# A table for the first-pass chunks, and small pieces spread over heads 1 to 3

## What is computed

```python
content = jnp.einsum('bqhd,bkhd->bhqk', q + u_bias, k)
pos_score = jnp.einsum('bqhd,khd->bhqk', q + v_bias, p)
pos_score = _rel_shift(pos_score)
score = (content + pos_score) / jnp.sqrt(jnp.float32(e))
attn = jax.nn.softmax(score, axis=-1)
ctx = jnp.einsum('bhqk,bkhd->bqhd', attn, v).reshape(b, s, e)
return ctx @ Wo + bo
```

## Time and profile before

| | |
|---|---|
| runs | 1982.84, 1982.9, 1983.7 us |
| profiled execution | 1981.65 us, its span 1979.9 us |
| TensorE busy | 1674.4 us, 85% |
| VectorE, ScalarE, POOL busy | 74%, 54%, 55% |
| attention loop | from about 100 to 1275 us of the span |
| granted TensorE clock, mean of the span | 0.892 |

### The profile page before, as it was taken

The page is one execution under the profiler, slowest core; times in us unless marked ns, Lnnn a source line. Parts: engine busy times, 40 slices in busy tenths (PEclk is TensorE's granted clock), DMA queues, the critical chain, the costliest instruction groups (busy, mean ns, idle before and its releaser), DMA issues. The chain is left out here.

```text
span 1979.9 us, 50794 instructions
## 1 busy us (share of the span) xinstructions
PE 1674.4 (85%) x12709; PEld 1283.0 (65%) x12710; DVE 1455.8 (74%) x5309; ACT 1068.1 (54%) x2080; POOL 1091.8 (55%) x2255
## 2 busy tenths in 40 slices
PE   3599999999999999999999999835444699999990
PEld 1366766766766766766766766634434599999990
DVE  4588788788788788788778788736555577777775
ACT  2067666666666666666666666501111465656553
POOL 4047546547547547547547547416877455555650
PEclk8599999999999999999999999955555799999995
DMA  4436436426426427327426426274221211111119
GB/s 167 127 95 155 107 85 159 110 77 164 112 70 172 111 64 177 109 64 174 109 71 167 109 81 165 75 236 116 65 65 42 67 53 52 51 53 53 52 49 257
DMA packets 167897, 212.14 MB, mean 107 GB/s; under 512 B 28049, under 2 KB 129313, under 8 KB 167681
## 3 DMA queue, kind: packets, MB, share of 16 engines
q1 hardware_dynamic: 137216, 149.63, 27.2%
q0 software_dynamic: 30464, 59.96, 12.2%
HBM read 127.01 MB, written 77.22 MB: 103 GB/s over the span
## 5 line engine op out<-in xcount | busy, mean ns | idle before, releaser
L778 DVE CUSTOM_DVE_ANT_0 junk<-pA,lmask 128x512 bf16<-128x512 f32 x1056 | 688.2, 683 | 224.5 <-PE pA L489 114.6
L720 ACT ACTIVATE prob<-pB 128x512 f32<-128x512 f32 x512 | 305.6, 597 | 194.0 <-PE pB L510 162.9
L722 ACT ACTIVATE prob<-pB 128x512 f32<-128x512 f32 x512 | 305.2, 596 | 1.3 <-PE pB L512 1.1
L489 PE MATMUL pA<-K,QL 96*128 96x512 f32 (+3 forms) x792 | 286.1, 363 | 19.9 <-DMA K<-split_operands 14.3
L528 PE MATMUL pC<-prob,vext 128*32 128x256 f32 x4112 | 283.8, 393 | 2.9 <-POOL prob L403 2.9
L403 POOL TENSOR_TENSOR prob<-prob,upper_diag 128x128 f32<-128x128 f32 x512 | 255.0, 498 | 47.8 <-POOL prob L398 10.5
L512 PE MATMUL pB<-QL,K 97*128 97x512 f32 (+3 forms) x768 | 279.4, 364 | 0.0
L510 PE MATMUL pB<-QU,K 97*128 97x512 f32 (+3 forms) x640 | 269.7, 421 | 7.4 <-ACT prob L720 2.8
L491 PE MATMUL pA<-K,QU 96*128 96x512 f32 (+3 forms) x660 | 235.9, 359 | 12.1 <-DVE acc L778 7.2
L396 POOL MEMSET prob<- 1x1 f32 x448 | 39.5, 88 | 345.6 <-ACT prob L722 345.5
L1471 POOL DMA_INDIRECT expert_rows<-yb,dst x144 | 158.2, 1098 | 102.5 <-DVE yb L1592 74.5
(11 more groups left out here) (272 smaller groups left out, 3437.7 us busy)
## 6 DMA issues: line engine op xcount, KB each, us to landing
QL<-split_operands SPq DMA_DIRECT2D x67, 256.0 KB, 3.5
QU<-split_operands SPq DMA_DIRECT2D x67, 256.0 KB, 3.9
K<-split_operands SPq DMA_DIRECT2D x67, 256.0 KB, 3.9
xg<-routed_rows SPq DMA_DIRECT2D x76, 130.0 KB
QL<-split_operands SPq DMA_DIRECT2D x67, 128.0 KB, 3.5
QU<-split_operands SPq DMA_DIRECT2D x67, 128.0 KB, 3.7
K<-split_operands SPq DMA_DIRECT2D x67, 128.0 KB, 3.7
split_operands<-c_h POOLq DMA_DIRECT2D x16, 512.0 KB, 6.4
```

The lines of the kernel that those rows point to most:

```text
L489: mm = pe.matmul(dst[:, 0:low], QL[0:KROWS, s, q], K[0:KROWS, s, k0:k0 + low], start=True, stop=True)
L720: act.activation(p[:, 0:HALF], pB[:, 0:HALF], ACT.Exp, scale=SCALE).then_inc(p_exp, 1)
L722: act.activation(p[:, HALF:S], pB[:, HALF:S], ACT.Exp, scale=SCALE).then_inc(p_exp, 1)
L778: v.tensor_tensor_reduce(junk[:, n % S1_BUFS, :], pA[n % S1_BUFS][:, :], lmask[:, at:at + HALF], 1.0, -3.0e38, ALU.add, ALU.max, acc[:, s, ...
```

## The change

The first-pass chunks of a unit are now taken from a table, `CHUNKS_AT`. In heads 0, 4, 5 and 7 (`PLAIN`) the nine units take 2, 1, 3, 2, 1, 3, 2, 3 and 1 chunks, in heads 1, 2, 3 and 6 (`EVEN`) two each. `ORDER` moves the diagonal chunk 16 to the third place of a head (unit 1) and 17 to the ninth (unit 4). Of an odd number above one, the rest goes behind the second half. The eight projections go from head 2's units 0 to 7 to the places of `PROJECT_AT`; "project 0/1", "shifted 0/1" and "values 0/1" move by one to four units, and what depends on them moves too: the splits, the positions, the stores and the swap.

```diff
-        M_ORDER.update({(1, 5): "project 1", (1, 7): "shifted 1", (6, 6): "values 0"})
-        W_ORDER = {(1, 0): "turn 0", (1, 2): "turn 1", (1, 4): "project 0", (1, 6): "shifted 0", (6, 5): "super", (6, 7): "values 1"}
+        M_ORDER.update({(1, 7): "project 1", (2, 2): "shifted 1", (6, 7): "values 0"})
+        W_ORDER = {(1, 0): "turn 0", (1, 2): "turn 1", (1, 5): "project 0", (2, 0): "shifted 0", (6, 5): "super", (7, 0): "values 1"}
+        PROJECT_AT = ((2, 3), (2, 5), (2, 7), (2, 8), (3, 0), (3, 2), (3, 3), (3, 5))
+        ORDER = (0, 1, 16, 2, 3, 4, 5, 6, 17, *range(7, 16))
+        EVEN, PLAIN = (2,) * S2U, (2, 1, 3, 2, 1, 3, 2, 3, 1)
+        CHUNKS_AT = {h: (EVEN if h in (1, 2, 3, 6) else PLAIN) for h in range(H)}
-        HIGH_AT = ((2, 5), (2, 6), (3, 0), (3, 1), (4, 1), (4, 2))
-        LOW_AT = ((2, 6), (2, 7), (3, 1), (3, 2), (4, 2), (4, 3), (4, 4), (4, 6))
+        HIGH_AT = ((3, 0), (3, 1), (3, 7), (3, 8), (4, 1), (4, 2))
+        LOW_AT = ((3, 1), (3, 2), (3, 8), (4, 0), (4, 2), (4, 3), (4, 4), (4, 6))
-        POSITIONS_AT = ((2, 7), (2, 8), (3, 1), (3, 3), (3, 5), (3, 7), (5, 2), (5, 4))
+        POSITIONS_AT = ((3, 3), (3, 4), (3, 6), (3, 7), (3, 8), (4, 0), (5, 2), (5, 4))
-        STORE_AT = {(3, 0): ("c", 0), (3, 2): ("c", 1), (3, 4): ("k", 0), (4, 4): ("gl", 0), (4, 7): ("gu", 0)}
+        STORE_AT = {(3, 5): ("c", 0), (4, 1): ("c", 1), (4, 2): ("k", 0), (4, 4): ("gl", 0), (4, 7): ("gu", 0)}
...
+        def chunks(h, u):
+
+            at, n = sum(CHUNKS_AT[h][:u]), CHUNKS_AT[h][u]
+            return [range(at, at + (n + 1) // 2), range(at + (n + 1) // 2, at + n)] if n < 3 else [range(at, at + 1), range(at + 1, at + n)]
...
+                    if h == 3:
+                        swap(b + 1)
                     if h == 2:
-                        swap(b + 1)
...
-                        second_pass(b, h, u, 0)
-                        first_pass(b, h + AHEAD, 2 * u)
-                        second_pass(b, h, u, 1)
-                        first_pass(b, h + AHEAD, 2 * u + 1)
-                        if (h, u) == (2, 0):
+                        for half in range(2):
+                            second_pass(b, h, u, half)
+                            for i in chunks(h, u)[half]:
+                                first_pass(b, h + AHEAD, i)
+                        if (h, u) == PROJECT_AT[0]:
                             pe.wait_ge(w_done, b * W_N + W_PRO + W_OF["shifted 0"] + 1)
-                        if h == 2 and u < PIECES:
-                            project(b + 1, u)
+                        if (h, u) in PROJECT_AT:
+                            project(b + 1, PROJECT_AT.index((h, u)))
...
-                        first_pass(b, h + AHEAD, 2 * u)
+                        first, *others = [i for half in chunks(h, u) for i in half]
+                        first_pass(b, h + AHEAD, first)
...
-                        first_pass(b, h + AHEAD, 2 * u + 1)
+                        for i in others:
+                            first_pass(b, h + AHEAD, i)
```

More of the change, by code:

```diff
@@ L475, in context_turned, with first_pass @@
                 return mm
-            def first_pass(b, h, n):
-                s = h % SLOTS
-                if n == 0:
+            def first_pass(b, h, i):
+                s, n = h % SLOTS, ORDER[i]
+                if i == 0:
                     pe.wait_ge(stk[s], b * (2 * STK) + (h // SLOTS + 1) * STK)
-                if not (isinstance(b, int) and h == 0 and n < S1_BUFS):
-                    pe.wait_ge(s1_read, b * (H * S1U) + h * S1U + n - S1_BUFS + 1)
-                dst = pA[n % S1_BUFS]
+                if not (isinstance(b, int) and h == 0 and i < S1_BUFS):
+                    pe.wait_ge(s1_read, b * (H * S1U) + h * S1U + i - S1_BUFS + 1)
+                dst = pA[i % S1_BUFS]
                 if n < NB * HPB:
@@ L492, in first_pass @@
                 else:
-                    for i in range(4):
-                        q = slice(P * (4 * (n % 2) + i), P * (4 * (n % 2) + i) + P)
-                        mm = pe.matmul(dst[:, P * i:P * i + P], QU[0:KROWS, s, q], K[0:KROWS, s, q], start=True, stop=True)
+                    for t in range(4):
+                        q = slice(P * (4 * (n % 2) + t), P * (4 * (n % 2) + t) + P)
+                        mm = pe.matmul(dst[:, P * t:P * t + P], QU[0:KROWS, s, q], K[0:KROWS, s, q], start=True, stop=True)
                 mm.then_inc(s1_ready, 1)
@@ L698, in _ @@
                         n = h * S2U + u
-                        if h == 2 and 0 < u <= PIECES:
-                            evacuate(b + 1, u - 1)
+                        before = (h, u - 1) if u else (h - 1, S2U - 1)
+                        if before in PROJECT_AT:
+                            evacuate(b + 1, PROJECT_AT.index(before))
                         if u == LATE:
@@ L706, in _ @@
                             act.activation(vext[:, :, H // 2:H, 0:D], held[:, :, :, :], ACT.Copy).then_inc(placed, 1)
-                        before = (h, u - 1) if u else (h - 1, S2U - 1)
                         if M_ORDER.get(before) in COPIES:
@@ L768, in super_out, with first_pass @@
                 v.tensor_tensor(acc[:, :, :, 3], src[:, 0:NB * H].rearrange("p (n h) -> p h n", h=H), cmask[:, :, :], ALU.add).then_inc(done, 1)
-            def first_pass(b, h, n):
-                s = h % H
-                pieces = known(v, b * (H * S1U) + h * S1U + n + 1)
+            def first_pass(b, h, i):
+                s, n, dst = h % H, ORDER[i], i % S1_BUFS
+                pieces = known(v, b * (H * S1U) + h * S1U + i + 1)
                 v.wait_ge(set_pool, POOL_SET)
@@ L777, in first_pass @@
                     at = 7 * P - P * qb + k0
-                    v.tensor_tensor_reduce(junk[:, n % S1_BUFS, :], pA[n % S1_BUFS][:, :], lmask[:, at:at + HALF], 1.0, -3.0e38, ALU.add, ALU.max,
+                    v.tensor_tensor_reduce(junk[:, dst, :], pA[dst][:, :], lmask[:, at:at + HALF], 1.0, -3.0e38, ALU.add, ALU.max,
                                            acc[:, s, qb, n % 2:n % 2 + 1]).then_inc(s1_read, 1)
@@ L781, in first_pass @@
                     g = n % 2
-                    for i in range(4):
-                        blk = 4 * g + i
-                        ttr = v.tensor_tensor_reduce(junk[:, n % S1_BUFS, P * i:P * i + P], pA[n % S1_BUFS][:, P * i:P * i + P], umask[:, :], 1.0, -3.0e38, ALU.add, ALU.max,
+                    for t in range(4):
+                        blk = 4 * g + t
+                        ttr = v.tensor_tensor_reduce(junk[:, dst, P * t:P * t + P], pA[dst][:, P * t:P * t + P], umask[:, :], 1.0, -3.0e38, ALU.add, ALU.max,
                                                      acc[:, s, blk, 2:3])
```

## The result

The changed kernel is **slower**: 2027.7 us median (2022.3 to 2037.7), the kernel before on the same chip 1982.9; ratio 1.0235, 95% interval 1.019 to 1.028. The forecast was 1958, the range 1938 to 1980. The profiled execution took 2029.55 us, its span 2027.9, mean granted clock 0.868 (before 0.892).

A forecast was written before the change was run, and what follows sets the result against it. It took VectorE to bound head 0 and an exp-and-matmul ring to bound quiet units without context. Terms of -2.55 us a batch, times 8, gave -20; clock -4; 1981.65 - 24.5 = 1957.2, median 1.25 higher: 1958, range 1938 to 1980.

The forecast's parts named there:

- I cost the stretch at nothing. The cover is VectorE's own backlog: Head 0 into head 1: VectorE is saturated, so the third chunks cost nothing; without that backlog the stretch would gain 0.5 us.
- 1.7 minus what the context of that unit hides is 1.1 net: Head 4: ScalarE's gl_h copy waits 1.7 us for POOL's position steps, 1.1 net; head 4 together +0.3 us.
- the clock falls at the new waits: Rival, chance 0.10: TensorE's fresh waits at (0,8) and (4,2) each cost 1.5 us a batch; 1977 us.
- The forecast's rule against it: Skill rule: idle gaps recurring in a loop re-throttle TensorE, so (0,8) and (4,2) would fall in every batch; 1977 us.
- clock term: Head 1: a third fewer clock drops expected, -4 us in all, bounds -9 and +12.
- The slower rival: Chance 0.12: the chain positions, gl, stores, stack becomes the loop's period; about 1994 us.
- stack wait of +0.6: Next batch's operands behind the gu store at (4,7): slack 0.7 us used up, +0.6 a batch charged, bounds 0 and 3.
- The pieces: Moved small pieces, us per batch: head 1 -1.4, head 2 -1.4, head 3 +1.4, values -0.25.
- The table in plain heads: Heads 0, 4, 5, 7: unit 8 -0.6, units 1 and 4 -0.2 each, read waits +0.55; a plain head gains about 0.5 us.
- The table in even heads: Heads 1, 2, 3, 6: unit 8 -0.4, units 1 and 4 +0.1 each; net -0.2 us a head.
- Wrong: Signs: head 5 unchanged, TensorE waiting over 2 us at head 6, gl_h over 4 us, or a lower mean loop clock.
- right: Signs: head 5 at most 15.4, its units 8 and 7 2.0 and 1.3; heads 1, 2, 3 19, 20.3, 19; gl_h waiting 1 to 2.

The follow-up runs named there:

- both repairs: Changed kernel with the residual add at (1,2) instead of (0,6), position steps at (3,3) to (3,8), first c store at (4,0): 1955.9 us, ratio 0.988.
- stores spread: Kernel with both repairs, its c stores put at (3,2) and (4,0) and its k store at (4,1): 1954.1 us, ratio 0.987.

## Why the prediction was wrong

- **"I cost the stretch at nothing. The cover is VectorE's own backlog"** (head 0): this step failed. I had the 2.61 us multiplication in the earlier trace rows and took it as its duration, though the addition of the same shape took 1.22. The 1.4 us between them was a meeting with POOL's residual add, whose place the table does not move but whose partner it does. After the change it meets the addition, with three reads and TensorE behind it. Cost: 7.6 us a batch in heads 0 and 1 (changed kernel against the one with the residual add moved). TensorE's stand, 2.76 us instead of 0.7, explains 2.1 of it; the rest came with the clock at 0.51 through the 12.67 us behind it. No run has the stand without the fall, so the two are not separated. The forecast had "about 1.2 us at (0,8)".
- **"1.7 minus what the context of that unit hides is 1.1 net"** (head 4): right mechanism, wrong size. Counted from the mask of (3,3) at 938.45, POOL took 16.2 us where 15.3 was summed (the upper select alone 1.54 for 1.1), and ScalarE stood at the copy after 13.2 instead of 13.6. The wait is 3.02 us, TensorE's share 2.26, and in five of eight batches the clock fell behind it. Head 4: +1.9 without the fall, +4.7 to +6.2 with it, forecast +0.3.
- **The rival "the clock falls at the new waits"** named both places and had 0.10. It priced a fall at 1.5 us from the earlier trace rows, where it lasted 3.4 us, behind two waits of TensorE of 0.62 and 0.69 us. After 2.76 us it lasted 10 to 14. The forecast's rule against it, a fall in every batch at both places, came true at the first (eight of eight) and not at the second (five of eight). Its sum of 1977 took the same short fall as a price. The forecast's own clock term was -4 us, for fewer falls; measured were 106 us more at the lower level.
- **The slower rival** named POOL's chain, the stores and the stack. The stack wait of +0.6 was not there in the changed kernel (head 6's first unit is 1.78 us as before in six batches, 1.80 and 2.21 in two); it appeared once the rest was faster. The port rule of the Trainium skill (page and section as cited above) was applied to the subtraction k_l at (4,0), and not to the pair that the trace already showed. At (4,0) it holds too, for a few tenths: k_l 0.92 us, POOL's upper select, begun inside it, 1.54 for 1.09.
- **The pieces** were near, except that head 3 cost less than charged. Head 1: -1.6 forecast, -2.0 measured (17.66 against the 19.67 of the kernel before with its residual add moved); head 2 -1.6 and -1.3; head 3 +1.2 and +0.6; heads 6 and 7 together, values among them, -0.95 and -0.1. Without the table on either side (two chunks to each unit and both repairs, against the kernel before with its residual add moved) the pieces are worth -1.7, -1.8 and +0.5 in heads 1, 2 and 3, where -1.4, -1.4 and +1.4 were forecast.
- **The table in plain heads**: -0.5 forecast, -0.26 measured in head 5. Unit 8 gave 0.51 of the 0.6; unit 3, behind a third chunk, took 0.36, as counted for the reads, unit 6 took 0.2 instead of 0.1, and unit 4 gave 0.1 of its 0.2.
- **The table in even heads**: -0.2 each forecast, which failed. With both repairs, and without falls of the clock, the table makes head 1 0.3 us shorter and heads 2, 3 and 6 0.5, 0.1 and 0.15 longer. With head 0, 0.2 longer, this uses up the 0.5 that heads 4, 5 and 7 gain together.

"Wrong" was to be TensorE over 2 us for operands, gl_h over 4 us, or a lower clock of the loop. The last came true in full (0.94 over 100 to 1275 us, before 0.98), the second in one batch of eight (4.49 us), the first not. Of the signs for "right", head 5's units 7 and 8 (1.26 and 2.13), head 2 (20.6) and head 3 (18.5) came near; head 5 as a whole (15.64), head 1 (21.6) and the wait for POOL did not. The forecast of 1958 is met by the kernel with both repairs (1955.9), but for another reason in part: its residual add had cost the kernel before 22 us (1983 against 1961). Taken from there, the pieces are worth some 18 us (1961.0 to 1943.3) and the table none.

Open: what delays the next batch's operands in two or three batches of a run. With the gu store one unit earlier the wait stayed. In all five kernels whose traces have it, the fourth and the seventh batch are among them. Open too is why one and the same wait of TensorE brings the clock down in some batches and kernels and not in others.

## What to carry to other kernels

When two instructions of the same shape on one engine differ in duration by a factor of two, find what the other engine does at that moment before moving anything: here the slow one was a meeting each time, and an edit that shifts either by some tenths can swap who waits. Price such a meeting by what stands behind the slowed instruction, not by its own microseconds: here 1.2 to 1.4 us on one instruction cost 0.9 to 3.0 us a batch (the most where the clock fell behind it), and 2.1 us on its neighbour 7.6. And a table that wins a quarter of a microsecond in quiet heads must be tried with the busiest head left out.

## What the runs showed of the hardware

- VectorE's tensor-tensor operations on vsh and POOL's additions exclude each other in both directions, and so do POOL's selects: 3.30 us for 1.22, 2.61 for 1.22, 1.48 for 0.46, 1.25 for 0.29. VectorE's reads of chunks from pA beside POOL's residual add kept their 0.68: in the kernel before, one that began 0.25 us into it took 0.69.
- The granted clock after a stand of TensorE: behind 2.76 us (head 0) it fell in all eight batches, during the stand or within 2 us of its end, to the 1.2 GHz level for 10 to 14 us; behind 2.26 us (head 4) in five of eight, for 3 to 10 us, and in seven of eight in the kernel that differs by the place of the residual add; behind 0.76, 0.58 and 0.85 us in one head (head 4, stores spread) in none. In the kernel before, a fall of 3.4 us came with 0.62 and 0.69 us in a row (head 1) in six of eight; with the pieces alone moved, the same two waits (about 0.62 and 0.68) stand in every batch and none has a fall. The same wait in the same place did and did not bring a fall, so a single price for it would be wrong.
